# A two-layer graph network on one core: nodes numbered eight to a partition in its unrolled path

## The reference, cut to what matters

```python
def L0(X, adj, W, b):
    deg = jnp.clip(jnp.sum(adj, axis=1, keepdims=True) + 1.0, 1.0, None)
    h_neigh = (adj @ X + X) / deg
    out = relu(jnp.concatenate([X, h_neigh], axis=1) @ W + b)
    return out / jnp.maximum(jnp.linalg.norm(out, axis=1, keepdims=True), 1e-12)

def L1(x, adj, W):
    for k in range(2):
        x = jnp.tanh(jnp.concatenate([adj @ x, x], axis=1) @ W[k])
    return x

x = layernorm(x + L0(x, adj, W0, b0))
x = layernorm(x + L1(x, adj, W1))
```

## Time and profile before

| | us |
|---|---|
| median of 3 runs | 1326.22 (1325.09 to 1327.84) |
| the profiled execution's own time | 1325.1 |
| its span | 1323.3 |
| stage 1 | 0 to about 800 |
| stage 2 | about 800 to 1323 |

### The profile page before, as it was taken

One profiled execution on the slowest core, in us unless ns is written; L12 is line 12 of the kernel. 1 busy time (PEld: TensorE's weight loads), 2 busy tenths in 40 slices (PEclk: granted clock), 3 DMA queues, 4 the chain that ended last, 5 costly groups with the idle time before them and its releaser, 6 DMA issues.

```text
span 1323.3 us, 25167 instructions
## 1 busy us (share of the span) xinstructions
PE 1200.9 (91%) x9450; PEld 816.9 (62%) x9450; DVE 1021.0 (77%) x2761; ACT 901.9 (68%) x1309; POOL 154.7 (12%) x118
## 2 busy tenths in 40 slices
PE   3779979989999999989999996999999999989886
PEld 2435646646546556546556555777787878777665
DVE  7888798898887887887787786884655555888996
ACT  5768778778777777777677653765555545877783
POOL 3000020010110110000110003240100000122221
PEclk9999999999999999999999998999999999999998
DMA  9999999999999999999899840000000000000000
GB/s 325 378 382 355 363 367 376 359 359 366 354 354 349 346 349 346 337 337 351 310 341 351 310 158 0 1 1 0 1 1 0 1 0 1 1 8 9 17 17 18
DMA packets 87818, 274.58 MB, mean 207 GB/s; under 512 B 22160, under 2 KB 22160, under 8 KB 87696
## 3 DMA queue, kind: packets, MB, share of 16 engines
q1 hardware_dynamic: 86656, 272.68, 56.1%
q10 hardware_dynamic: 1040, 0.26, 0.1%
HBM read 270.83 MB, written 2.10 MB: 206 GB/s over the span
## 4 chain that ended last, share of the span: by engine, by line
PE 66%; DVE 13%; issue 7%; DMA 6%; POOL 5%; ACT 2%; DVEq 0%; POOLq 0%; ACTq 0%
PE acc L678 29%; PE acc L842 21%; PE ps_pack L669 7%; DMA raw<-in_adj 6%; DVE marks L911 5%; PE ps_epi L707 4%; DVE planes L929 2%; ACT raw L440 2%; PE ps_pack L804 2%; PE ps_pack L802 2%; POOL root L561 1%; DVE packed L916 1%; POOL root L557 1%; PE ps_epi L817 1%; DVE wide L1100 1%
## 5 line engine op out<-in xcount | busy, mean ns | idle before, releaser
L440 ACT ACTIVATE raw<-raw 128x1024 f32<-128x1024 uint32 x512 | 535.7, 1048 | 206.0 <-DVE marks L911 205.0
L678 PE MATMUL acc<-planes,feats 128*128 128x512 fp8e4 x2512 | 567.8, 381 | 7.8 <-issue 7.8
L678 PEld LDWEIGHTS acc<-planes,feats 128*128 128x128 bf16 x2512 | 238.4, 98 | 278.6 <-issue 14.9
L479 ACT ACTIVATE wide<-twos 128x2048 fp32r<-128x2048 fp8e4 x150 | 284.2, 1916 | 160.0 <-PE acc L842 127.1
L911 DVE TENSOR_SCALAR marks<-raw 128x2048 uint8<-128x2048 f32 x256 | 312.6, 1240 | 21.5 <-DMA raw<-in_adj 19.8
L1100 DVE TENSOR_SCALAR wide<-twos 128x2048 fp32r<-128x2048 uint8 x150 | 184.9, 1233 | 78.6 <-PE acc L842 77.7
L669 PE MATMUL ps_pack<-pow,marks 128*128 128x64 bf16 x4096 | 143.3, 194 | 58.0 <-DVE marks L911 57.9
L669 PEld LDWEIGHTS ps_pack<-pow,marks 128*128 128x128 fp8e4 x4096 | 137.2, 99 | 81.4 <-issue 73.9
L1086 DVE TENSOR_SCALAR twos<-packed 128x128 uint32<-128x128 uint32 x600 | 124.6, 270 | 60.8 <-ACT wide L479 53.8
L929 DVE TENSOR_SCALAR planes<-packed 128x128 uint32<-128x128 uint32 x1024 | 150.8, 220 | 23.0 <-DVE packed L916 22.2
L842 PE MATMUL acc<-wide,x_high 128*128 128x512 f32 x512 | 130.0, 400 | 13.3 <-DVE wide L1100 12.9
(11 more groups left out here) (130 smaller groups left out, 872.9 us busy)
## 6 DMA issues: line engine op xcount, KB each, us to landing
raw<-in_adj SPq DMA_DIRECT2D x256, 1024.0 KB, 6.2
out<-result SPq DMA_DIRECT2D x8, 256.0 KB, 2.6
zpart<-in_x SPq DMA_DIRECT2D x7, 256.0 KB, 8.0
zpart<-in_x ACTq DMA_DIRECT2D x1, 256.0 KB, 9.3
w_own<-in_L_gnn_W SPq DMA_DIRECT2D x8, 16.0 KB, 6.5
w_a<-in_L_gnn_W SPq DMA_DIRECT2D x4, 16.0 KB, 6.9
w_y<-in_L_gnn_W SPq DMA_DIRECT2D x2, 16.0 KB, 6.8
w_x<-in_L_gnn_W SPq DMA_DIRECT2D x2, 16.0 KB, 6.9
```

Source lines behind the costliest of these rows:

```text
L440: ins = act.activation(words, words.bitcast(U32), ACT.Sign, accum_out=nonzero[:, tile:tile + 1, I])
L479: act.activation(out_ap, twos[:, u % 2].bitcast(F8), ACT.Abs).then_inc(low_ready, 1)
L678: mm = pe.matmul(acc[g][:, h, :], feats[g][:, I * TB + a, :], planes[:, h, a, :], start=(start or g in opens) and a == 0, stop=a == TB - 1 ...
```

## The change

In the unrolled path, tile t of a block and partition p now hold node p * 8 + t: eight neighbouring nodes lie on one partition. The four places are the view of the adjacency rows, the view of the result, the load of `x`, and the weights of `pack`.

```diff
--- before.py
+++ after.py
@@ -156,8 +156,8 @@
 
 
 def gnn_kernel(nc, x, adj, w0, b0, w1, out):
-    adj_t = adj.rearrange("(j q p) (i c) -> j i p q c", q=TB, p=P, c=BLK)
-    out_t = out.rearrange("(j t p) d -> j p t d", t=TB, p=P)
+    adj_t = adj.rearrange("(j p q) (i c) -> j i p q c", q=TB, p=P, c=BLK)
+    out_t = out.rearrange("(j p t) d -> j p t d", t=TB, p=P)
 
     with ExitStack() as ctx:
         def sb(name, shape, dt):
@@ -369,7 +369,7 @@
 
         def load_x(eng, I):
 
-            eng.dma_start(tiles(zpart[:, I, :]), x[I * BLK:(I + 1) * BLK, :].rearrange("(t p) d -> p t d", p=P)
+            eng.dma_start(zpart[:, I, :], x[I * BLK:(I + 1) * BLK, :].rearrange("(p t) d -> p (t d)", p=P)
                           ).then_inc(xin_landed[I], 16)
 
         block = ctx.enter_context(nc.Block())
@@ -666,7 +666,8 @@
                 pass_wait(pe)
                 for a in range(TB):
                     for q in range(QH):
-                        mm = pe.matmul(ps_pack[:, a * NW:(a + 1) * NW], marks[:, h, q, a * P:(a + 1) * P],
+                        columns = marks[:, h, q, :].rearrange("p (m a) -> p a m", a=TB)[:, a]
+                        mm = pe.matmul(ps_pack[:, a * NW:(a + 1) * NW], columns,
                                        pow2[:, q, :], start=q == 0, stop=q == QH - 1)
                 mm.then_inc(pack_done, 1)
```

## The result

| | before | changed |
|---|---|---|
| median, us (10 runs each) | 1325.11 (1319.2 to 1327.84) | 1335.63 (1328.51 to 1338.26) |
| ratio to before | | 1.008, 95% interval 1.0059 to 1.0101 |
| profiled execution, its own time / span | 1325.1 / 1323.3 | 1332.09 / 1330.2 |

One execution on record stands apart, one of 4336.65 us among the ten of experiment 2; ratios are worked out without it.

A forecast was written before the change was run, and what follows sets the result against it. Stage 1 was taken as DMA-bound until about 90 us, later TensorE-bound. From the 1326.2 us median, 1.7 us (x 1.2, last store 0.5) came off: 1324.5 us; forecast's own range 1321 to 1329, 8-in-10 range 1315 to 1400.

The forecast's parts named there:

- Every eighth byte: Packing weight loads on TensorE, read at a step of 8 bytes: hidden behind the 29 ns matmul, costing nothing.
- The load rival: Every pack on the chain: strided load no longer hides, 0.76 us more on each of 95 packs, 1397 us; chance 0.20.
- The rule of the Trainium skill: Packing weight loads: weights read 32 bits at a time, so columns take four times as long, 137 us; within 0.04 chance.
- x in 2 KB pieces: Six later x loads in the DMA-bound loop of stage 1: 0.2 us saved each, 1.2 us (0 to 3.0).
- The result: Stage 2's result stores in 2 KB pieces: only the last, which ends the kernel, saves 0.5 us.
- The adjacency pieces: Stage 1's adjacency loads: same 65536 pieces of 4 KB from other addresses, 0 us.
- The pieces were merged: x and result transfers: some 16000 fewer packets under 512 B; the unmerged rival, 1326.2 us, had chance 0.05.

The follow-up runs named there:

- experiment 2: The changed kernel with packing weights read side by side again, the new addresses and 2 KB pieces kept: 1322.43 us, ratio 0.999.
- runs 1 and 2: The kernel before with only packing weights read every eighth byte, 1334.48 us; and the changed kernel with weights side by side again, 1322.43 us.
- run 5: The kernel before with x and result in 2 KB pieces, adjacency addresses and packing weights unchanged: 1323.31 us, ratio 0.999.

## Why the prediction was wrong

The forecast was 1324.5 us, no change; measured were 1335.63.

**Where it failed: "Every eighth byte ... I take 0, and the load may even grow by half before it shows."** The term was put at nothing and is 0.13 to 0.14 us a pack: a pair takes 33 ns and not 29. The column part of a load did not grow by half at most but doubled, from 19 ns (99 - 80) to 38 (118 - 80), past the 29 ns of a pair. The argument was that time goes by columns, because one and two bytes a weight take 98 and 99 ns. Those two points touch 8 and 16 lines, and the runs are flat up to 32: both lay on the flat part and could not tell a law by columns from one by lines. The float32 row, 32 lines and 111 ns, was the only other one, and it differs in more than lines (32 lines of one-byte weights take 99 ns). A step no row shows had been given the value of the nearest flat rows.

**The load rival had the mechanism and the sign, not the size.** Its place (the packs of the chain) and its point (29 ns of columns) held: 24 ns at a step of 6 is hidden, 38 at 8 is not. That the column part paces the pair one for one does not hold, though: it is 38 ns at a step of 8 and 87 at 16, and the pairs take 33 and 60. Its price, 0.76 us a pack, came from a pack after an idle wait, which did not change with the load (the changed kernel's same row is 1.87 us); the surcharge measured 0.13 to 0.14. Its count of 95 packs held about as well as can be told: the losses of 9.8 to 14.9 us in the 111 steps are 73 to 110 such surcharges, and the medians of runs 1 and 2 give some 75 to 90. With the measured 0.135 the rival's own sum would have been 1324.5 + 95 x 0.135 = 1337 us instead of 1397.

**The sum of what happened**, in the two profiled executions: +14.9 us in 111 steps, -3.8 in the first block, 11.1 at the end of stage 1; -0.7 for the last store. That this comes to 10.4 where the medians differ by 10.5 is partly luck: the first two terms carry a scatter of 5 and 2 us, and the spans differ by only 6.9.

**The rule of the Trainium skill** ("TensorE: Matmul & The Clock Gate", weight-path perf modes: weights read 32 bits at a time), as the prediction read it, would have cost at steps of 2 and 4 already, and 137 us at 8. Neither happened, so its size was rightly rejected; that a strided load costs at all was rejected with it, and wrongly. The Trainium skill's note on cachelines ("SBUF — State Buffer", specifications) names the right unit, 16-byte lines, and steps of 16 and 32 at one price bear it out. That two hits in a line bring full speed does not hold here: at a step of 8 there are two, and the load is 19 ns longer.

**x in 2 KB pieces: 1.2 us forecast, 1.1 to 3.8 measured** at the end of block 0 (run 5), so the term was rather too low than too high, and the runs do not refute it. I had set the saving low since 379 GB/s with x loads was more than 369 without. The shares in the same rows, 1.05 and 1.01, said that the engines were busier for it: 361 GB/s at a share of one, and x in large pieces gives 389 / 1.02 = 381 (run 5).

**The result: 0.5 us forecast, 0.7 measured** (3.1 to 2.4 us of landing). **The adjacency pieces: 0 forecast, none measured.** The pieces were merged, 16384 fewer packets under 512 B (22160 to 5776), as foretold.

The time lies inside the stated range of 1315 to 1400, but only because that reached to the overpriced rival; it is outside the forecast's own 1321 to 1329. The side was wrong.

## What to carry to other kernels

A rearrangement of data moves a stride from one access to another; find out for each engine that now reads or writes at a step whether that access is hidden, and by how much. Here 128 one-byte weights are free to load up to a step of 6 bytes under a matmul of 64 columns, cost 4 ns a pair at 8 and 31 at 16. A flat row in the trace bounds only the part of the law it lies on: before taking it for the new value, ask what both share (here, lines touched).

## What the runs showed of the hardware that I had not expected

- The time of a weight load of 128 one-byte columns goes by the 16-byte lines that they touch (the line is the Trainium skill's unit, named above): 99 ns up to 32 lines, 104 at 48, 118 at 64, 167 and 168 at 128. The steps of 6, 16 and 32 are one execution each.
- VectorE's conversion from float32 to bytes takes 4.98 us instead of 1.24 for 2048 elements when neighbouring elements are written 128 bytes apart.
- The same 256 adjacency rows, in 1 MB loads of the same piece size, landed after 7.8 us (median) instead of 6.2 when each partition took two consecutive rows and the partitions followed one another in HBM, and held SyncE 540 ns instead of 368; this cost 0.9%, and issuing each load in two took it away.
